# Tokens of a mixture-of-experts layer scattered and gathered once, as doubled rows ordered by pair of keeping experts

## The chip, the cores and the metric

The kernel runs on one core of one Trainium2 chip. The metric is the time of one execution on the device in microseconds; lower is better.

## What is computed

Two layers follow each other on images of 128 channels. The first is a 7x7 depthwise convolution, a norm over the channels and a mixture of eight experts with capacity; the second is an attention by coordinates with a 3x3 convolution, whose input is the first one's output. Cut to what matters here:

```python
x = depthwise_conv7x7(input) + dw_bias             # (32, 128, 56, 56)
x = layernorm(x over channels) * ln_gamma + ln_beta
xf = x.reshape(T, C)                               # T = 100352 tokens, C = 128
topv, topi = top_k(xf @ Wg + bg, 2)                # 8 experts, 2 per token
wts = softmax(topv)
order = argsort(-wts[:, 0])                        # priority
cap = int(1.25 * T / 8)                            # 15680 rows per expert
# in order of priority each expert keeps its first cap tokens
h = gelu(einsum('ecd,edf->ecf', eb, W1) + b1)      # 128 -> 512
y = einsum('ecf,efd->ecd', h, W2) + b2             # 512 -> 128
moe = sum over the 2 picks of y[slot] * gate       # gate 0 where not kept
z = input + x + layer_scale * moe
# second layer, per image: means over rows and columns -> 8 channels ->
# h_swish -> two sigmoids a_h, a_w; conv3x3(z * a_w * a_h), batch norm, SiLU
```

All values are fp32. A token is kept by two experts, by one or by none.

## The kernel before

The program is a row of blocks; each ends with a barrier of all engines. The work of each engine stands in its own function, in order, with semaphores between the engines.

**conv_norm_phase** does the depthwise convolution as matrix products with Toeplitz matrices, stores it to DRAM, reads it back turned, norms it and stores the normed tokens to `xn`, 112 chunks of 896 tokens (128 partitions x `CHK` = 7 tokens of 128 channels). It also leaves the routing logits in SBUF.

**route_phase** finds on DVE the two picks of each token, then by bisection (24 steps, DVE with ACT and PE) the priority that each expert's last kept token has, and by scans the slot of each pick: expert e keeps its tokens in rows e x 15680 and on of `xe`, in order of the chunks. Slots of picks that aren't kept lie outside, and the indirect DMAs leave them out. SP meanwhile fills `xe` with zeros (L504, 16 DMAs). The slots of the first 14 chunks are made first (`early_set`); POOL waits for the zeros and for them, and scatters the first `EARLY` = 8 chunks while DVE makes the other slots. DVE also counts, for each expert and tile of 448 rows, after how many scattered chunks the tile is full (`needed`).

**Scatter.put** (L435) is one chunk's scatter on POOL: wait for the chunk's load, start the load of a later one (L418), then 7 x 2 indirect DMAs, one for each token of a partition and each pick, each of 128 rows of 512 bytes. The last thing in it is the wait for the chunk before to have landed, and the count `chunks_scattered` goes up.

**expert_phase** works on 35 tiles of each expert, 448 rows each, the eight experts in turn: 280 turns, the first and last eight written out and the others in a loop over q with eight turns in its body. POOL scatters the other 104 chunks, with a fill `lull` of 3000 elements after each (L805). SP's queue does, in each turn, `load(t + 5)`: wait for a free buffer, read `needed[q, e]` from SBUF into a register (`value_load`, L823), wait for that many chunks, and one DMA of 224 KB from `xe` (L825); then `store(t)`: wait for the result, one DMA of 224 KB to `ye` (L831). PE's turn is four products up (L875), the turning of the next tile's rows to columns (L866), four products down for the tile before (L883) and the turning back (L892); ACT does the Gelu, DVE the copies out of PSUM.

**output_phase** works on 16 pairs of images, 7 chunks each. POOL gathers for chunk n with 7 x 2 indirect DMAs (L1117) from `ye` into `y_ring`, seven chunks deep; in the first pair it fills the chunk's part of the ring with zeros first (L1113), since rows of tokens that weren't kept aren't written. DVE multiplies by the gates and adds to the normed tokens (L1293), PE turns the chunk (L1170), DVE adds it to the image (L1306); after chunks 3 and 6 come the means, the attention (PE L1180, L1183, L1184; ACT's sigmoid; DVE L1336 and L1338 write `padded`), and PE's 3x3 convolution of the image, seven banks of nine products (L1150), is laid between the next chunks by the list `BEHIND`. The order on every engine is written out by hand.

Of the kernel before, what the change touches and what calls it, by code (L numbers as in the profile page):

```python
# [7 lines left out]
U32 = mybir.dt.uint32  # L8
ALU = mybir.AluOpType
# [3 lines left out]
C = 128  # L13
# [6 lines left out]
E = 8  # L20
# [8 lines left out]
EARLY_PAIRS = 2  # L29
EARLY = 8  # L30
LULL = 3000


def plan(n_images):

    tokens = n_images * HW
    cap = int(1.25 * tokens / E)
    pairs = n_images // 2
    tiles = 35
    tm = cap // (tiles * BLOCKS)  # L40
    assert tm * tiles * BLOCKS == cap and tm <= 128
    return dict(N=n_images, T=tokens, CAP=cap, PR=pairs, J=pairs * KT, TM=tm, TILES=tiles, DROP=E * cap)
# [37 lines left out]
def conv_norm_phase(nc, s, x, dw_kernel, dw_bias, bands, conv, xn, ln_gamma, ln_beta, Wg, bg, logits):  # L80
# [26 lines left out]
    with ExitStack() as ctx:  # L107
# [138 lines left out]
        def _(dve):  # L246
# [20 lines left out]
            def make_hat(m):  # L267
# [17 lines left out]
                dve.tensor_tensor(logits[:, :, m * CHK:(m + 1) * CHK].rearrange("p e j -> p j e"), off[q][:],  # L285
# [113 lines left out]
class Scatter:  # L399


    RING = 7

    def __init__(self, nc, ctx, s, xn, xe, slots):
        sb = lambda name, shape, dt=F32: ctx.enter_context(nc.sbuf_tensor(name, shape, dt))
        sem = lambda name: ctx.enter_context(nc.semaphore(name))
        self.xn, self.xe, self.slots = xn, xe, slots
        self.chunks = s["PR"] * NCHK
        self.chunk = [sb(f"chunk{i}", [128, CHK * C]) for i in range(self.RING)]
        self.chunk_in = [sem(f"chunk_in{i}") for i in range(self.RING)]  # L410
        self.scattered = [sem(f"scattered{i}") for i in range(self.RING)]
        self.chunks_scattered = sem("chunks_scattered")

    def load(self, pool, n):

        g, ch = divmod(n, NCHK)
        i = n % self.RING
        pool.dma_start(self.chunk[i][:], self.xn[g * 128:(g + 1) * 128, ch * CHK * C:(ch + 1) * CHK * C]  # L418
                       ).then_inc(self.chunk_in[i], 16)

    def landed(self, pool, n):

        turn, i = divmod(n, self.RING)
        pool.wait_ge(self.scattered[i], (turn + 1) * 2 * CHK * 16)
        pool.sem_inc(self.chunks_scattered, 1)

    def put(self, pool, n, limit):

        turn, i = divmod(n, self.RING)
# [14 lines left out]
def route_phase(nc, s, logits, xe, slots, gates, needed, scatter):  # L444

    PR, J, CAP, DROP, TILES = s["PR"], s["J"], s["CAP"], s["DROP"], s["TILES"]
# [3 lines left out]
    ZP, ZR, ZD = 98, 80, 16  # L453
    assert ZP * ZR * ZD == E * CAP
    GR = PR * NCHK
    SLICES = ((0, EARLY_PAIRS * NCHK), (EARLY_PAIRS * NCHK, GR))

    with ExitStack() as ctx:
        sb = lambda name, shape, dt=F32: ctx.enter_context(nc.sbuf_tensor(name, shape, dt))
        sem = lambda name: ctx.enter_context(nc.semaphore(name))  # L460
        pick = [sb(f"pick{c}", [128, E, J], BF16) for c in range(2)]
        prio, work = (sb(n, [128, E, J]) for n in ("prio", "work"))
        scan = sb("scan", [128, E * J + 2])
        junk = sb("junk", [128, E, J], BF16)
        zeros = sb("zeros", [ZP, 4 * C])
        top = [sb(f"top{c}", [128, J]) for c in range(2)]
        first, rel = (sb(n, [128, J]) for n in ("first", "rel"))
        ones, below, one_row = sb("ones_r", [128, 128]), sb("below", [128, 128]), sb("one_row", [128, 1])
        bound, low, cand, count, hit, need, minus_mid, enough = (
            sb(n, [128, E]) for n in ("bound", "low", "cand", "count", "hit", "need", "minus_mid", "enough"))  # L470
        flat_logits = logits[:].rearrange("p e j -> p (e j)")
# [925 lines left out]
```

## Time and profile before

| | us |
|---|---|
| median of 3 runs | 5972.66 |
| lowest, highest | 5960.88, 5988.47 |
| span of the profiled execution | 6004.2 |

| engine | busy us | share of the span |
|---|---|---|
| PE | 4869.7 | 81% |
| POOL | 3488.9 | 58% |
| DVE | 2405.2 | 40% |
| ACT | 1512.5 | 25% |

The profile is of one execution, which took 31.5 us more than the median of the runs. The chain that the page shows runs back from the last instruction, at each step to what released it. Instructions of a sequencer (register work, table reads, branches, the issue of DMAs by SP) aren't counted as busy; SP has no row in the table for that reason.

### The profile page before, as it was taken

What the parts mean: (1) busy time and instruction counts of PE and PEld (TensorE: products, weight loads), DVE (VectorE), ACT (ScalarE), POOL (GpSimd) and SP (SyncE); (2) the same over time, 40 slices, a digit from 0 to 9 for tenths busy, and PEclk for the clock granted to TensorE, in tenths of its full rate; (3) what the DMA queues carried; (4) which work ended last, traced back from release to release, by engine and by line L of the source; (5) the groups of instructions that cost most, each with busy time, mean ns of one, the idle gap of its engine ahead of it and who ended that gap; (6) DMA issues with size and microseconds to landing.
All of it is one profiled execution on the core that took longest, in us unless ns stands there. A gap on an engine that the chain in (4) does not pass through costs nothing. (4 is left out here: it accounts for less than half of the span.)

```text
span 6004.2 us, 66408 instructions
## 1 busy us (share of the span) xinstructions
PE 4869.7 (81%) x20680; PEld 2721.7 (45%) x20680; DVE 2405.2 (40%) x4770; ACT 1512.5 (25%) x3688; POOL 3488.9 (58%) x3508
## 2 busy tenths in 40 slices
PE   8999999310399997998779878558888888888888
PEld 3555658310255554544445444224444444444444
DVE  0012226896022222222222222356656556556553
ACT  2233336350033332333223323101111111111111
POOL 0000000004777777877777777477777777777773
PEclk9999999655599998999889989779999999999999
DMA  8887779863333333333223322323333322222310
GB/s 168 185 182 196 194 180 248 260 205 112 96 117 118 118 113 96 94 88 98 84 83 90 93 83 75 118 93 102 105 104 103 107 92 85 82 88 86 101 61 33
DMA packets 840398, 711.26 MB, mean 118 GB/s; under 512 B 596072, under 2 KB 681710, under 8 KB 836090
## 3 DMA queue, kind: packets, MB, share of 16 engines
q1 hardware_dynamic: 666362, 466.30, 28.6%
q0 software_dynamic: 109312, 139.69, 8.5%
q10 hardware_dynamic: 64512, 102.79, 5.0%
q8 instruction: 91, 1.49, 0.1%
q14 instruction: 121, 0.99, 0.0%
HBM read 440.11 MB, written 385.75 MB: 138 GB/s over the span
## 5 line engine op out<-in xcount | busy, mean ns | idle before, releaser
L1117 POOL DMA_INDIRECT y_ring<-ye,index_o x1568 | 1580.7, 1008 | 462.2 <-issue 460.3
L435 POOL DMA_INDIRECT xe<-chunk,slots x1568 | 1536.4, 980 | 476.8 <-issue 476.8
L1150 PE MATMUL cp<-padded,taps_o 128*128 128x448 f32 x4032 | 1627.3, 561 | 62.4 <-DVE padded L1338 62.4
L1150 PEld LDWEIGHTS cp<-padded,taps_o 128*128 128x128 f32 x4032 | 782.1, 198 | 811.8 <-issue 777.6
L921 ACT ACTIVATE hid<-hid_ps,b_cols 128x448 f32<-128x448 f32 x1120 | 709.3, 633 | 1489.6 <-PE hid_ps L875 1391.3
L883 PE MATMUL y_ps<-hid,w_sb 128*128 128x448 f32 x2240 | 932.7, 561 | 0.4 <-DVE yt L946 0.4
L875 PE MATMUL hid_ps<-xt,w_sb 128*128 128x448 f32 x2240 | 890.9, 541 | 1.5 <-DVE xt L940 1.5
L513 POOL MEMSET zeros<- 98x512 f32 x1 | 0.5, 524 | 1109.2 <-POOLq L107 1109.2
L1216 ACT ACTIVATE outb<-cp,shift,s 128x448 f32<-128x448 f32 x224 | 162.1, 724 | 1757.7 <-PE cp L1150 1757.6
L883 PEld LDWEIGHTS y_ps<-hid,w_sb 128*128 128x128 f32 x2240 | 423.1, 199 | 336.4 <-issue 335.8
L1293 DVE SCALAR_TENSOR_TENSOR logits<-y_ring,gates,logits 128x128 f32<-128x128 f32 x1568 | 432.6, 345 | 353.9 <-DMA y_ring<-ye,index_o 336.9
L940 DVE COPY xt<-xt_ps 128x448 f32<-128x448 f32 x280 | 174.8, 624 | 970.3 <-PE xt_ps L866 962.5
L363 PE MATMUL cv<-xin,toep 56*56 56x448 f32 x5376 | 540.0, 543 | 15.8 <-ACT rows L308 9.5
L875 PEld LDWEIGHTS hid_ps<-xt,w_sb 128*128 128x128 f32 x2240 | 404.9, 191 | 315.9 <-issue 311.2
L946 DVE TENSOR_SCALAR yt<-y_ps,b_cols,scale_col 128x448 f32<-128x448 f32 x280 | 208.3, 744 | 691.9 <-PE y_ps L883 691.9
L375 PEld LDWEIGHTS ps<-turner,pix 128*128 128x128 f32 x1568 | 366.8, 326 | 49.1 <-issue 39.9
L375 PE MATMUL ps<-turner,pix 128*128 128x136 f32 x1568 | 378.0, 399 | 8.5 <-DMA pix<-conv 8.5
L1170 PE MATMUL tp<-ident_o,logits 128*128 128x128 f32 x784 | 133.6, 322 | 308.0 <-DVE logits L1293 308.0
L866 PE MATMUL xt_ps<-ident_e,rows_in 112*128 112x112 f32 x1120 | 165.0, 272 | 232.2 <-DMA rows_in<-xe 232.0
L363 PEld LDWEIGHTS cv<-xin,toep 56*56 56x56 f32 x5376 | 224.1, 126 | 284.8 <-issue 262.2
L270 DVE RECIPROCAL rstd<-std 128x7 f32<-128x7 f32 x112 | 22.5, 201 | 818.8 <-ACT std L331 818.8
L1306 DVE SCALAR_TENSOR_TENSOR summed<-tp,beta_o,summed 128x896 f32<-128x896 f32 x112 | 205.4, 1834 | 288.3 <-PE tp L1170 288.2
(198 smaller groups left out, 3627.4 us busy)
## 6 DMA issues: line engine op xcount, KB each, us to landing
xe<-zeros SPq DMA_DIRECT2D x16, 3920.0 KB
rows_in<-xe SPq DMA_DIRECT2D x280, 224.0 KB, 2.7
ye<-rows_out SPq DMA_DIRECT2D x280, 224.0 KB, 2.3
xin<-in_x_dram SPq DMA_DIRECT2D x256, 196.0 KB
conv<-rows ACTq DMA_DIRECT2D x256, 196.0 KB
pix<-conv SPq DMA_DIRECT2D x224, 224.0 KB, 5.1
xn<-hat SPq DMA_DIRECT2D x112, 448.0 KB, 4.3
chunk<-xn POOLq DMA_DIRECT2D x112, 448.0 KB, 3.7
```

The lines of the kernel that those rows point to most:

```text
L363: last = pe.matmul(bank(t, half)[blk * TWO:blk * TWO + H, 0:BW], toep[half * TWO:half * TWO + H, i, kw, :], xin[t % XB][half * TWO:half * ...
L375: last = pe.matmul(tile(m, j), strips[:, j:j + 127 * CHK + 1:CHK], turner[:], start=True, stop=True)
L435: pool.indirect_dma_start(out=self.xe[:, :], out_offset=bass.IndirectOffsetOnAxis(ap=self.slots[:, c, n * CHK + j:n * CHK + j + 1], axis=0 ...
L875: pe.matmul(hid_ps[f][:, 0:NT], w1_sb[e][:, f * 128:(f + 1) * 128], xt[e % 2][:], start=True, stop=True).then_inc(hid_done, 1)
L883: last = pe.matmul(y_ps[:, 0:NT], w2_sb[e][:, f, :], hid[e % 2][:, f, :], start=(f == 0), stop=(f == NH - 1))
L921: act.activation(hid[e % 2][:, f, :], hid_ps[f][:, 0:NT], ACT.Gelu, bias=b1_cols[:, e * NH + f:e * NH + f + 1]).then_inc(hid_ready, 1)
L940: dve.tensor_copy(xt[e % 2][:], xt_ps[e % 2][:, 0:NT]).then_inc(xt_ready, 1)
L946: dve.tensor_scalar(yt[e % 2][:], y_ps[:, 0:NT], b2_cols[:, e:e + 1], scale_col[:, 0:1], ALU.add, ALU.mult).then_inc(yt_ready, 1)
L1117: pool.indirect_dma_start(out=y[ch][c][:, j * C:(j + 1) * C], out_offset=None, in_=ye[:, :], in_offset=bass.IndirectOffsetOnAxis(ap=index[ ...
L1150: last = pe.matmul(cp[i % 2][:, 0:HB * W], taps[:, t, :], padded[b][:, img, hb * HB + kh:hb * HB + kh + HB, kw:kw + W], start=(t == 0), st ...
L1293: last = dve.scalar_tensor_tensor(part, y[ch][c][:, j * C:(j + 1) * C], gates[:, c, bass.ds(n * CHK + j, 1)], part, ALU.mult, ALU.add)
L1306: dve.scalar_tensor_tensor(part, tp[q][:, 0:CC].rearrange("c (k t) -> c k t", k=CHK), beta_c[:, 0:1], part, ALU.add, ALU.add).then_inc(add ...
```

## The change

- The tokens are put into 37 classes: one for each pair of experts a < b that both keep the token, one for each single expert, one for none. Each class fills whole blocks of 128 rows of one DRAM tensor `xy`, whose rows are doubled: 2 x 128 channels. Only each class's last block, and the blocks outside the used ones, are zeroed.
- Each token has one slot. POOL copies a chunk to a doubled one (`twice`), and scatters it with 7 indirect DMAs of 128 rows of 1 KB. Tokens that nobody keeps are scattered too.
- Expert a of a pair reads the left half of a block's rows and overwrites it with its result, expert b the right half. Each expert has up to 130 blocks, taken in the order in which the chunks fill them: 33 tiles of four blocks (the last of two), 512 columns. Where the blocks are stands in a table `where`, read from SBUF, one entry for each block's load and one for its store.
- The output phase gathers each token's row once, 1 KB, and has both results. The gates are exchanged where the second pick is the lower expert (`split_gates`, DVE, in the experts' fifth turn).
- route_phase is rewritten after the bisection: each token's code of keeping experts, flags of the 37 classes, their counts by PE products in bf16, the class starts, the slots of the first 13 chunks, then the table, then the other slots.
- `lull` and the filling of `y_ring` go.

The scatter:

```diff
     def put(self, pool, n, limit):
-        turn, i = divmod(n, self.RING)
-        pool.wait_ge(self.chunk_in[i], (turn + 1) * 16)
-        if n + self.RING - 2 < self.chunks:
-            self.load(pool, n + self.RING - 2)
+        i, d = n % self.STAGED, n % self.DOUBLED
+        pool.wait_ge(self.chunk_in[i], (n // self.STAGED + 1) * 16)
+        if n >= self.DOUBLED:
+            pool.wait_ge(self.scattered[d], (n // self.DOUBLED) * CHK * 16)
+        pool.tensor_copy(self.twice[d][:], self.chunk[i][:].unsqueeze(2).to_broadcast([128, CHK, 2, C])).then_inc(self.copied, 1)
+        pool.wait_ge(self.copied, n + 1)
+        if n + self.STAGED < self.chunks:
+            self.load(pool, n + self.STAGED)
         for j in range(CHK):
-            for c in range(2):
-                pool.indirect_dma_start(
-                    out=self.xe[:, :],
-                    out_offset=bass.IndirectOffsetOnAxis(ap=self.slots[:, c, n * CHK + j:n * CHK + j + 1], axis=0),
-                    in_=self.chunk[i][:, j * C:(j + 1) * C], in_offset=None,
-                    bounds_check=limit, oob_is_err=False).then_inc(self.scattered[i], 16)
+            at = j * self.chunks + n
+            pool.indirect_dma_start(
+                out=self.xy[:, :], out_offset=bass.IndirectOffsetOnAxis(ap=self.slots[:, at:at + 1], axis=0),
+                in_=self.twice[d][:, j, :, :].rearrange("p h c -> p (h c)"), in_offset=None,
+                bounds_check=limit, oob_is_err=False).then_inc(self.scattered[d], 16)
         if n:
             self.landed(pool, n - 1)
```

The experts' loads and stores on SP:

```diff
+                at = [sp.value_load(tables.where[0:1, bass.ds(q * BLOCKS + k, 1), 0, e:e + 1].rearrange("p q e -> p (q e)"),
+                                    min_val=0, max_val=2 * ROWS - 256 + 1) for k in range(blocks)]
-                sp.wait_ge(chunks_scattered, sp.value_load(needed[0:1, bass.ds(q, 1), e:e + 1].rearrange("p q e -> p (q e)"),
+                sp.wait_ge(chunks_scattered, sp.value_load(tables.chunks[0:1, bass.ds(q, 1), e:e + 1].rearrange("p q e -> p (q e)"),
                                                            min_val=1, max_val=PR * NCHK))
-                sp.dma_start(rows_in[i][0:TM, :, :], xe[bass.ds(e * CAP + q * NT, NT), :]
-                             .rearrange("(p k) c -> p k c", k=BLOCKS)).then_inc(tile_in[i], 16)
-
-            def store(t, e, q):
+                for k in range(blocks):
+                    sp.dma_start(rows_in[i][:, k, :], halves[bass.ds(at[k], 256), :].rearrange("(p h) c -> p h c", h=2)[:, 0, :]
+                                 ).then_inc(tile_in[i], 16)
+
+            def store(t, e, q, blocks):
                 i = e % RING
                 sp.wait_ge(out_ready, t + 1)
-                sp.dma_start(ye[bass.ds(e * CAP + q * NT, NT), :].rearrange("(p k) c -> p k c", k=BLOCKS),
-                             rows_out[i][0:TM, :, :]).then_inc(tile_out[i], 16)
+                for k in range(blocks):
+                    at = sp.value_load(tables.where[0:1, bass.ds(q * BLOCKS + k, 1), 1, e:e + 1].rearrange("p q e -> p (q e)"),
+                                       min_val=0, max_val=2 * ROWS - 256 + 1)
+                    sp.dma_start(halves[bass.ds(at, 256), :].rearrange("(p h) c -> p h c", h=2)[:, 0, :], rows_out[i][:, k, :]
+                                 ).then_inc(tile_out[i], 16)
```

The output phase's gather:

```diff
-                    if first:
-
-                        pool.memset(y_ring[:, ch * 2 * CC:(ch + 1) * 2 * CC], 0.0).then_inc(cleared, 1)
-                        pool.wait_ge(cleared, ch + 1)
                     for j in range(CHK):
-                        for c in range(2):
-                            pool.indirect_dma_start(
-                                out=y[ch][c][:, j * C:(j + 1) * C], out_offset=None, in_=ye[:, :],
-                                in_offset=bass.IndirectOffsetOnAxis(ap=index[ch][:, c, j:j + 1], axis=0),
-                                bounds_check=limit, oob_is_err=False).then_inc(y_in[ch], 16)
+                        pool.indirect_dma_start(
+                            out=y[ch][:, j, :, :].rearrange("p h c -> p (h c)"), out_offset=None, in_=xy[:, :],
+                            in_offset=bass.IndirectOffsetOnAxis(ap=index[ch][:, j:j + 1], axis=0),
+                            bounds_check=limit, oob_is_err=False).then_inc(y_in[ch], 16)
```

The new parts of route_phase on which the steps rest (the last block of each class is zeroed by SP for one half of the classes and by ACT for the other; flags and placing on DVE):

```diff
+        def clear_tails(eng, c0, c1):
+
+            for c in range(c0, c1):
+                at = eng.value_load(tails_u[0:1, c:c + 1], min_val=0, max_val=ROWS - 128)
+                eng.dma_start(xy[bass.ds(at, 128), :], zeros[:]).then_inc(zeroed, 16)
...
+            for c0, c1 in SUM_GROUPS:
+                for c in range(c0, c1):
+                    last = dve.tensor_scalar(flags[:, c], code, float(codes[c]), None, ALU.is_equal)
+                last.then_inc(flags_set, 1)
...
+                for c in range(c0, c1):
+                    do(dve.copy_predicated(place[:, :, g0:g1], flags[:, c, :, g0:g1].bitcast(U16),
+                                           ranks[:, c - c0, :].unsqueeze(1).to_broadcast([128, CHK, G])))
```

## Rows read from the trace of the kernel before

**Rows 1.** The page: busy time by engine, and its chain by engine.
```profile
PE 4869.7 (81%) x20680; PEld 2721.7 (45%) x20680; DVE 2405.2 (40%) x4770; ACT 1512.5 (25%) x3688; POOL 3488.9 (58%) x3508
...
POOL 27%; issue 8%; PE 1%; DVE 0%; POOLq 0%; DMA 0%; ACT 0%; ACTq 0%
```

**Rows 2.** Stages: window, length, each engine's busy time (x instructions), clock, DMA.
```profile
0.00:1110.00 1110.00, 1070.57 (x8740) 678.67 (x8740) 281.42 (x1246) 437.05 (x2002) 0.88 (x8) 0.99 0.83 197
1110.00:1419.00 309.00, 42.72 (x134) 33.56 (x134) 284.76 (x542) 103.57 (x210) 6.95 (x28) 0.51 0.66 215
...
1584.00:3835.00 2251.00, 1991.66 (x6786) 1096.45 (x6786) 550.71 (x843) 710.77 (x1122) 1741.98 (x1666) 0.94 0.33 97
3835.00:6004.00 2169.00, 1764.74 (x5020) 913.02 (x5020) 1241.91 (x2087) 261.07 (x355) 1616.55 (x1688) 0.90 0.29 92
```

**Rows 3.** POOL's groups, 1584 to 3770: count | busy, mean ns | idle.
```profile
L435 POOL DMA_INDIRECT xe<-chunk,slots x1456 | 1418.0, 974 | 442.7 <-issue 442.7
L805 POOL MEMSET lull<- 128x3000 f32 x104 | 273.5, 2630 | 0.0
L418 POOL DMA_DIRECT2D chunk<-xn x99 | 59.6, 602 | 0.3 <-issue 0.3
```

**Rows 4.** Waits, 1584 to 3835: total, times, longest.
```profile
PE xt_ps L866 <- DMA rows_in<-xe: 232.0, 24, 27.5
```

**Rows 5.** Timeline of PE, one turn of the experts: start, length.
```profile
1687.15 3.17 PE L875 MATMUL hid_ps<-xt,w_sb 128*128 128x448 f32 x8
1690.16 0.55 PE L866 MATMUL xt_ps<-ident_e,rows_in 112*128 112x112 f32 x4
...
1694.00 3.17 PE L875 MATMUL hid_ps<-xt,w_sb 128*128 128x448 f32 x8
```

**Rows 6.** POOL's groups, 3835 to 6004.
```profile
L1117 POOL DMA_INDIRECT y_ring<-ye,index_o x1568 | 1580.7, 1008 | 462.2 <-issue 460.3 <-POOL y_ring L1113 1.9
```

**Rows 7.** Timeline of PE, output: between two attention products.
```profile
4850.80 0.36 PE L1180 MATMUL ap<-pooled,w_t 128*8 128x112 f32 x2
...
4868.38 13.79 PE L1150 MATMUL cp<-padded,taps_o 128*128 128x448 f32 x36 [1.96 <-DVE padded L1338]
...
4903.94 0.36 PE L1180 MATMUL ap<-pooled,w_t 128*8 128x112 f32 x2
```

**Rows 8.** Timeline of PE: first convolution of the output phase.
```profile
3948.84 15.28 PE L1150 MATMUL cp<-padded,taps_o 128*128 128x448 f32 x36 [5.04 <-DVE padded L1338]
```

**Rows 9.** Timelines: DVE's last early slots, POOL's first load after the zeros.
```profile
1347.64 0.21 DVE L741 TENSOR_SCALAR slots<-rel 128x98 uint32<-128x98 f32 x1
...
1418.18 0.54 POOL L418 DMA_DIRECT2D chunk<-xn  x1 [300.81 <-DMA xe<-zeros]
```

**Rows 10.** Timeline of DVE: bf16 passes, a scan, fp32 passes.
```profile
1124.34 4.17 DVE L600 TENSOR_TENSOR pick<-pick,junk 128x784 bf16<-128x784 bf16 x7
...
1354.04 11.59 DVE L685 TENSOR_TENSOR_SCAN scan<-total,work 128x5488 f32<-128x5488 f32 x1
...
1385.01 6.36 DVE L710 TENSOR_TENSOR work<-work,junk 128x686 f32<-128x686 f32 x8
```

**Rows 11.** Timeline of SP's queue: loads with constant tiles, a store, a load.
```profile
1598.04 4.93 SPq L825 DMA_DIRECT2D rows_in<-xe  x6
...
1702.14 0.33 SPq L831 DMA_DIRECT2D ye<-rows_out  x1
1703.35 0.32 SPq L825 DMA_DIRECT2D rows_in<-xe  x1
```

**Rows 12.** SP's instructions of L823 and L825: count, ns min/median/max.
```profile
L823 SPq FUSED_REGOPS  x544: 46/147/187, 1597.7 to 3798.4; - x182
L823 SPq TENSOR_LOAD <-needed x280: 269/281/975, 1597.2 to 3798.1; - x140
...
L825 SPq DMA_DIRECT2D rows_in<-xe x280: 312/322/350, 1598.0 to 3798.7; - x140
...
DMA to landing us min/median/max: 2.4/2.7/5.9
```

More of the change, by code:

```diff
@@ L38, in plan @@
     pairs = n_images // 2
[L39 to L42, printed above, removed]
+    blocks = (cap + E * 127) // 128
+    assert (TILES - 1) * BLOCKS < blocks <= TILES * BLOCKS and tokens == 784 * 128
+    return dict(N=n_images, T=tokens, CAP=cap, PR=pairs, J=pairs * KT, LAST=blocks - (TILES - 1) * BLOCKS)
 class Steps:
@@ L440, in put, with __init__ @@
         if n:
             self.landed(pool, n - 1)
-def route_phase(nc, s, logits, xe, slots, gates, needed, scatter):
-    PR, J, CAP, DROP, TILES = s["PR"], s["J"], s["CAP"], s["DROP"], s["TILES"]
+class Picks:
+    def __init__(self, nc, ctx, s, gates):
+        sb = lambda name, shape, dt=F32: ctx.enter_context(nc.sbuf_tensor(name, shape, dt))
+        J = s["J"]
+        self.top = [gates[:, c, :] for c in range(2)]
+        self.code, self.code0 = (sb(n, [128, J], BF16) for n in ("code", "code0"))
@@ L450, in route_phase, with __init__, class_of @@
+class Tables:
+    def __init__(self, nc, ctx, s):
+        sb = lambda name, shape, dt: ctx.enter_context(nc.sbuf_tensor(name, shape, dt))
+        self.where = sb("where", [128, POSITIONS, 2, E], U32)
+        self.chunks = sb("chunks_of_tile", [128, TILES, E], U32)
+def class_of(a, b):
+    return a * E - a * (a - 1) // 2 + b - a
+def route_phase(nc, s, logits, xy, slots, picks, tables, scatter):
+    PR, J, CAP = s["PR"], s["J"], s["CAP"]
     GROUPS = 2
@@ new lines, in route_phase @@
+        slots_k = slots[:].rearrange("p (k g) -> p k g", k=CHK)
+        first, rel = (sb(n, [128, J]) for n in ("first", "rel"))
+        place = first[:].rearrange("p (k g) -> p k g", k=CHK)
+        same, inner = (rel[:].bitcast(BF16)[:, i * J:(i + 1) * J].rearrange("p (k g) -> p k g", k=CHK) for i in range(2))
+        ones, ones_b = sb("ones_r", [128, 128]), sb("ones_b", [128, 128], BF16)
+        below_b = sb("below_b", [128, 128], BF16)
+        bound, low, cand, count, hit, need, minus_mid, enough, weight = (
+            sb(n, [128, E]) for n in ("bound", "low", "cand", "count", "hit", "need", "minus_mid", "enough", "weight"))
@@ L580, in _ @@
+            last.then_inc(table_summed, 1)
+            for i in range(len(low_bank), NRG):
+                class_ranks(i)
         @block.vector
@@ L651, in _ @@
             last.then_inc(above_counted, 1)
+            prio_k, pick0_k, junk_k = by_chunk(prio), by_chunk(pick[0]), by_chunk(junk[:])
+            dve.wait_ge(ramps_set, 1)
+            dve.memset(tab, 0.0)
+            dve.memset(inner[:, 0, :], 0.0)
+            dve.memset(place, 0.0)
+            do(dve.memset(ahead[:, :, 0, :], 0.0))
+            for e in range(E):
+                last = dve.tensor_scalar(tie[:, e], prio_k[:, e], bound[:, e:e + 1], 2.0 ** e, ALU.is_equal, ALU.mult)
+            last.then_inc(ties_set, 1)
@@ new lines, in rank_within, with set_slots @@
+            def rank_within(g0, g1):
+                for d in range(1, CHK):
+                    out = inner[:, 1:, g0:g1] if d == 1 else same[:, 0:CHK - d, g0:g1]
+                    do(dve.tensor_tensor(out, code[:, d:, g0:g1], code[:, 0:CHK - d, g0:g1], ALU.is_equal))
+                    if d > 1:
+                        do(dve.tensor_tensor(inner[:, d:, g0:g1], inner[:, d:, g0:g1], same[:, 0:CHK - d, g0:g1], ALU.add))
+            def set_slots(g0, g1):
+                do(dve.tensor_tensor(slots_k[:, :, g0:g1], place[:, :, g0:g1], inner[:, :, g0:g1], ALU.add))
@@ L973, in output_phase @@
-def output_phase(nc, s, x, xn, ye, ln_beta, slots, gates, logits, out, p):
+            scale(end - 1, E - 1, False, LAST * 128)
+            result(end - 2, E - 2, TILES - 1, False, LAST)
+            result(end - 1, E - 1, TILES - 1, False, LAST)
+def output_phase(nc, s, x, xn, xy, ln_beta, slots, gates, logits, out, p):
     PR, N = s["PR"], s["N"]
```

680 lines of the change are left out of this document (435 added, 245 removed).

## The prediction

> **What bounds the kernel now.** I read the page first, for the order of things: PE is busy 81% of the span, and yet the chain that ended last is mostly POOL's, on one line, the gather of the output phase [rows 1]. Then the busy time by stage [rows 2]: the first 1110 us (convolution and norm) are PE's and are left alone by the change; then come the routing (1110 to 1419), POOL's first eight puts, which close the route block (1419 to 1584), the experts (1584 to 3835, 2251 us) and the output (3835 to 6004, 2169 us).
>
> Experts: POOL's groups in that stage show 1456 indirect scatters of 0.974 us with 0.30 us of issue between them, and 104 fills `lull` of 2.63 us [rows 3]. 104 chunks x (14 x 1.28 + 2.63 + 0.4) = 104 x 21.0 = 2180 us, and PE's only large wait is for tiles that the scatter had not filled, 232 us [rows 4]. A turn of PE is 6.85 us when it doesn't wait [rows 5], 280 x 6.85 = 1918. So the scatter sets this stage's end, with PE 15% behind. Output: 1568 gathers of 1.008 us at a pitch of 1.30 [rows 6], 14 per chunk, 112 x 18.4 = 2060 us of 2169. PE needs less: between two attention products, in a half pair in which nothing waited for a gather, lie 53.1 us [rows 7], about 107 us for a pair where gathering takes 129.
>
> **The output phase.** Each chunk now takes 7 gathers, 7 x 1.30 + 0.4 = 9.5 us, 33 us for half a pair against PE's 53: POOL leaves the path and PE's own order of work is what is late next. First convolution: it starts at 3948.8 now [rows 8], 114 us into the stage, behind four chunks of 20 us (the ring's fills of 1.5 us go too). With 9.5 us each it starts 74 us in. From there PE has 32 images x 48.0 (7 banks of 6.86), 107 chunks' transposes x 0.77 = 82, 31 attention products x 0.87 = 27, the wait of about 1.9 us per image for `padded` that the rows show, 57 [rows 7], and 10 before the last image: 1712, and 4 at the end. 74 + 1712 + 4 = 1790 against 2169: **-379 us**. Bounds: if DVE's and ACT's turns hold a pair at 115 instead of 107 us, -250; below 107 it can't go, as PE's work is the same.
> Does one gather of 1 KB rows cost what one of 512 B rows does? No row shows 1 KB rows. The scatter and the gather take 0.97 and 1.0 us whatever lies in their slots, so I take 1.0, the nearest rows; upper end twice that (a rival below).
>
> **The route block.** The zeroing of `xe` (62 MB) goes, and POOL waited for it until 1418.2, although DVE had the early slots at 1347.9 [rows 9]. In its place DVE must finish all classes' counts before the first slot. Working on from the end of the search (1319.4), with a bf16 pass of 784 at 0.6, a fp32 pass of 686 at 0.80 and a scan at 2.1 ns an element [rows 10]: 16 compares 9, `ahead` 4, tie run 3, `taken` 6.4, two bf16 passes 8, `code` 3.5, 37 flags x 0.3 = 11, the wait for PE's and ACT's class sums 16 (it hides `inner` and `code0`), block arithmetic 6, 37 predicated copies x 0.3 = 11: 78, so slots at about 1398, then the 36 tail clears, 18 on SP and 18 on ACT at 0.92, overlap it and end near 1404. POOL then makes 8 puts; each is 7 x 1.28, the load 0.9 and the doubling copy. No row shows a copy on POOL; it writes 1792 elements, 1.6 us at the fill's rate [rows 3], at most some 4: I take 2.5, and 15 us for a put while DVE works beside it. 1404 + 120 + 9 for the end of the block = 1533; DVE's late part (scan 9, table 45, 37 copies x 0.9 = 34) ends near 1490, under it. The experts start **51 us earlier**; bounds -80 and +20, as half of these operations have no row of their own.
>
> **The experts, PE's side.** Blocks are full 128 rows, 130 per expert: 8 x 130 x 128 = 133120 columns against 125440. The eight large products of a turn are 6.02 us for 448 columns [rows 5], so 6.88 for 512, and the transposes 0.85: 7.7 us a turn, 256 of them and 8 of half size, 2000 us, 80 more than before. The scatter: a put is 7 x 1.28 + 0.9 + 2.5 = 12.4 us, 104 puts in 1290 us; the `lull` goes. It no longer holds PE.
>
> **The experts, SP's side.** This is what is late next. SP did one table read and two DMAs a turn; now it does nine reads and eight DMAs, all in one in-order queue: a tile's load is four block loads, its store four block stores, each with its own address from `where`. What one costs is in SP's timeline: from a store's issue to the next load's issue, with one table read between them and nothing to wait for, 1.21 us in the loop (1702.14 to 1703.35), and 0.92 us where the tile number is a constant (six loads issued in 4.93 us, the last taking 0.32: 4.61/5) [rows 11]. The parts are there too: the read 0.28, its check 0.147 at the median, the DMA itself 0.32 [rows 12]. A block thus costs between 0.92 and 1.21; I take 1.16, near the loop's value, since addresses come from the loop's register, less a little because the new reads' lower limit is 0. A turn: 8 x 1.16 + 0.62 for the ninth read = **9.9 us, more than PE's 7.7**. The cover that hid SP's work before (it waited most of each 6.85 us) is gone. Sum of the stage: 14 for the weights' DMAs, 21 for the first five loads, 8 turns with constants x 7.9 = 63, 240 in the loop x 9.9 = 2376, again 63, the half turns 22, the end 10: 2569 against 2251, **+318 us**. Store waits don't add to it: a store comes five loads behind its own tile. The scatter's count is ready: eight tiles take 79 us and need 3.4 chunks, 42 us.
>
> The Trainium skill, DMA: Bandwidth & Descriptors, section on latency and other measured facts, puts a floor of about 600 ns under a table read (`tensor_load`). The trace disagrees: 281 ns at the median of 280 [rows 12]; with 600 the turn would be 12.8 us. The same page, under issuing engines that are not separate queues, says that the time to start a DMA is usually small beside the DMA itself, which speaks against an SP bound; of one DMA that holds here too, 0.32 us of issue and 2.7 to landing [rows 12]. Eight of them overlap in landing and not in issue, so I weigh the issue.
>
> **Other parts.** The new order of `logits` and `slots` changes strides only, 0 (off DVE's path in the first 1110 us). Splitting the gates is 11 short DVE operations in the fifth turn of the experts: DVE is busy 551 of 2251 us [rows 2], 0. Half-row blocks make four DMA pieces of each 2 KB one; the DMA engines are 33% busy in that stage [rows 2], 0 on the path. The clock: a PE that waits 2 us a turn may be granted less; it was granted 0.94 in this stage with long waits [rows 2], and at 0.9 a turn is still under 9.9.
>
> **Sum.** -51 + 318 - 379 = -112 us on the profiled 6004.2. The median of the runs is 5972.7, 31.5 below the profile, so 5973 - 112 = **5861 us**, -1.9%.
>
> **Rivals.**
> A, slower: SP's turn is dearer. At 1.21 a block, with the ninth read at 0.66 and 0.3 a turn for the loop's branch and the fetch of a body five times as long (SP's dearest read took 975 ns where the median is 281 [rows 12]), it is 10.6 us: +170, **6031 us**. For it: the loop rows are those of the same queue. Against: that row has a check against two limits. Slower than before begins at 9.9 + 112/240 = 10.4 us a turn.
> B, SP is cheap: at 0.92 a block, 7.9 us, SP and PE are level. -2.0 x 240 = -480, **5380 us**. For it: the constant-address rows; against: only where no register is needed.
> C, a doubled row costs twice: scatter 1.94, gather 2.0 us. Puts in the route block +54; in the experts 104 x 19.3 = 2010, hidden by SP; the gather 112 x 16.4 + 105 = 1940 against 1790, +150: **6065 us**. Against it: a load of 3.5 KB rows on the same engine costs POOL 0.60 us [rows 3], so the bytes of a row aren't what POOL pays for.
> D, PE's order isn't as tight as in the half pair I read: 115 us a pair, +128, **5989 us**, no change.
> E, the table read at the skill's 600 ns. Worked out from rows it is a read twice as long: its dearest, 975, is rare; at 281 + 300, 9 x 0.3 = 2.7 more a turn, +648, **6509 us**. The skill's figure (page above) is about that.
> F, the change doesn't shorten POOL's gather, because dropped tokens, which were skipped, are now fetched: the count of instructions, not of rows, sets 1.3 us, so this is C in small, and is in it.
>
> **Chances.** Forecast 62% (own range 5740 to 5985), A 17%, B 8%, C 5%, D 7%, E 1%. A measurement tells about 0.5%, 30 us, from no change. Faster: 0.55 of the forecast, B, 0.01 of D: 0.64. Within: 0.05 of the forecast, 0.02 of A, 0.05 of D: 0.12. Slower: 0.02 of the forecast, 0.15 of A, C, E and 0.01 of D: 0.24. To leave no more than 2 in 10 out, the range goes from 5640 (a turn of 9.0) to 6080 (through A and C).
>
> **What would show it.** In the profile after: SP's DMA issues in the experts' loop without a gap, turns of 9.9 us, PE waiting about 2 us in each for `rows_in` and no longer for POOL; the scatter done some 1000 us before the stage ends; in the output phase POOL idle half of the time, pairs of 107 us and the chain on PE; the first scatter near 1404 and the experts' start near 1533. Wrong: turns of 7.7 with PE at work throughout (B), indirect DMAs near 2 us (C), or a route block past 1600.

## The result, and the profile after

The changed kernel takes 7259 us (7256 to 7261, four runs) against 5967 (5957 to 5988): a ratio of **1.215 [1.212, 1.219]**. It is much slower, where 5861 was forecast and the range ended at 6080. The profiled execution has a span of 7257.9 us, 1254 more than the one of before.

The page of the kernel after, busy time by engine and the chain by engine (beside [rows 1]):

```profile
PE 5066.4 (70%) x20517; PEld 2657.6 (37%) x20517; DVE 2421.7 (33%) x4879; ACT 1540.1 (21%) x3769; POOL 1893.5 (26%) x1983
...
PE 20%; DVE 4%; issue 1%; ACT 1%; ACTq 0%
```

POOL has 1983 instructions where it had 3508 and is off the chain, as meant. Busy time by stage, same columns as [rows 2]; the lines are the norm, the route block, POOL's early puts, a stretch that before did not have, the experts' turns, and the output:

```profile
0.00:1110.00 1110.00, 1069.97 (x8740) 678.29 (x8740) 281.63 (x1246) 438.27 (x2002) 0.89 (x8) 0.99 0.84 197
1110.00:1419.00 309.00, 62.79 (x263) 40.27 (x264) 296.65 (x641) 121.89 (x355) 61.12 (x83) 0.55 0.17 58
1419.00:1541.00 122.00, 23.03 (x193) 19.41 (x192) 54.05 (x104) 0.00 (x0) 91.91 (x92) 0.50 0.44 147
1541.00:2722.00 1181.00, 26.19 (x68) 12.17 (x68) 4.98 (x7) 12.17 (x17) 915.92 (x901) 0.51 0.35 117
2722.00:5447.00 2725.00, 2198.88 (x6236) 1034.76 (x6236) 549.84 (x796) 706.29 (x1040) 0.00 (x0) 0.94 0.17 50
5447.00:7258.00 1811.00, 1685.50 (x5020) 872.70 (x5020) 1234.60 (x2087) 261.50 (x355) 823.67 (x900) 0.96 0.43 143
```

From 1541 to 2722 hardly anything but POOL works: PE is busy 26 of 1181 us. The waits of SP's queue (in total, times, longest) name the reason, and PE's timeline shows its two holes:

```profile
SPq L1064 <- POOLq L434: 1180.1, 2, 735.9
```

```profile
1966.66 1.08 PE L1109 MATMUL xt_ps<-ident_e,rows_in 128*128 128x128 f32 x4 [429.25 <-DMA rows_in<-xy]
...
1990.90 3.60 PE L1117 MATMUL hid_ps<-xt,w_sb 128*128 128x512 f32 x8
2722.26 1.12 PE L1109 MATMUL xt_ps<-ident_e,rows_in 128*128 128x128 f32 x4 [727.77 <-DMA rows_in<-xy]
```

SP waits twice for `chunks_scattered` (POOL's increments, L434). It has read the table for its first tile at 1518 and may load it at 1962.8; three tiles follow at once, and the fifth, expert 4's first, comes at 2718.9. POOL's scatters up to the first of these moments, and in all (count: ns min/median/max, first and last start):

```profile
L448 POOL DMA_INDIRECT xy<-twice,slots x331: 971/976/1332, 1402.6 to 1961.5; - x166
```

```profile
L448 POOL DMA_INDIRECT xy<-twice,slots x784: 968/976/1332, 1402.6 to 2716.2; - x196
```

At seven scatters a chunk, 331 are 47 chunks and a little of the 48th; the last of the 784 starts at 2716.2, 2.6 us before the fifth tile's load. So the table asked for 47 of 112 chunks for the first tile and for **all 112** for the fifth. In the kernel before, PE waited 232 us in all for tiles [rows 4], and SP 530.7 us, in 27 waits, for the same count:

```profile
SPq L825 <- POOLq L425: 530.7, 27, 39.2
```

Between the waits and the output lies SP's queue. Its timeline over a round of eight turns (start, length; the lines between are alike):

```profile
3398.21 1.94 SPq L1064 DMA_DIRECT2D rows_in<-xy  x4
3401.08 3.92 SPq L1073 DMA_DIRECT2D xy<-rows_out  x4
3408.82 1.94 SPq L1064 DMA_DIRECT2D rows_in<-xy  x4
...
3470.45 1.96 SPq L1064 DMA_DIRECT2D rows_in<-xy  x4
3473.33 3.87 SPq L1073 DMA_DIRECT2D xy<-rows_out  x4
3483.58 1.94 SPq L1064 DMA_DIRECT2D rows_in<-xy  x4
```

3398.21 to 3483.58 is 85.4 us for eight turns, **10.67 us a turn**: seven of 10.3 on average and, at the loop's end, one of 13.1. SP has no gap in them, and PE waits about 2 us in each (1675.8 us of waits for `rows_in` less the two holes is 519, over 238 turns).

### The profile page after: what moved, and what is told of

Read it like the earlier page. It is cut to its first block and busy times, and to the rows that moved or that the text cites. A ratio compares the mean times of both kernels' runs of the same rounds, so it can differ in the third digit from the quotient of the medians.

```text
span 7257.9 us, 77541 instructions
## 1 busy us (share of the span) xinstructions
PE 5066.4 (70%) x20517; PEld 2657.6 (37%) x20517; DVE 2421.7 (33%) x4879; ACT 1540.1 (21%) x3769; POOL 1893.5 (26%) x1983
## 3 DMA queue, kind: packets, MB, share of 16 engines
q0 software_dynamic: 84224, 257.01, 10.9%
## 5 line engine op out<-in xcount | busy, mean ns | idle before, releaser
L1413 PE MATMUL cp<-padded,taps_o 128*128 128x448 f32 x4032 | 1578.3, 547 | 62.5 <-DVE padded L1601 62.5
L1109 PE MATMUL xt_ps<-ident_e,rows_in 128*128 128x128 f32 x1040 | 182.4, 300 | 1676.3 <-DMA rows_in<-xy 1675.8
L1167 ACT ACTIVATE hid<-hid_ps,b_cols 128x512 f32<-128x512 f32 (+1 forms) x1056 | 717.2, 681 | 2748.5 <-PE hid_ps L1117 2747.0
L1125 PE MATMUL y_ps<-hid,w_sb 128*128 128x512 f32 (+1 forms) x2112 | 1078.6, 660 | 0.4 <-DVE yt L1192 0.4
L1186 DVE COPY xt<-xt_ps 128x512 f32<-128x512 f32 (+1 forms) x264 | 180.4, 684 | 2516.9 <-PE xt_ps L1109 2516.9
L1117 PE MATMUL hid_ps<-xt,w_sb 128*128 128x512 f32 (+1 forms) x2112 | 939.2, 587 | 3.0 <-DVE xt L1186 3.0
L1380 POOL DMA_INDIRECT y_ring<-xy,index_o x784 | 799.2, 1019 | 244.2 <-issue 241.1
L448 POOL DMA_INDIRECT xy<-twice,slots x784 | 770.0, 982 | 255.9 <-issue 255.1
L1109 PEld LDWEIGHTS xt_ps<-ident_e,rows_in 128*128 128x128 f32 x1040 | 117.0, 148 | 1887.2 <-DMA rows_in<-xy 1453.9
L1192 DVE TENSOR_SCALAR yt<-y_ps,b_cols,scale_col 128x512 f32<-128x512 f32 (+1 forms) x264 | 211.7, 802 | 833.4 <-PE y_ps L1125 833.4
```

Source lines behind the costliest of these rows:

```text
L448: pool.indirect_dma_start(out=self.xy[:, :], out_offset=bass.IndirectOffsetOnAxis(ap=self.slots[:, at:at + 1], axis=0), in_=self.twice[d][ ...
L1109: last = pe.transpose(xt_ps[e % 2][:, k * 128:(k + 1) * 128], rows_in[e][:, k, :], ident[:])
L1117: pe.matmul(hid_ps[f][:, 0:cols], w1_sb[e][:, f * 128:(f + 1) * 128], xt[e % 2][:, 0:cols], start=True, stop=True).then_inc(hid_done, 1)
L1125: last = pe.matmul(y_ps[:, 0:cols], w2_sb[e][:, f, :], hid[e % 2][:, f, 0:cols], start=(f == 0), stop=(f == NH - 1))
L1167: act.activation(hid[e % 2][:, f, 0:cols], hid_ps[f][:, 0:cols], ACT.Gelu, bias=b1_cols[:, e * NH + f:e * NH + f + 1]).then_inc(hid_ready, 1)
L1192: dve.tensor_scalar(yt[e % 2][:, 0:cols], y_ps[:, 0:cols], b2_cols[:, e:e + 1], scale_col[:, 0:1], ALU.add, ALU.mult).then_inc(yt_ready, 1)
```

## The experiments

The theory, **O**: the two long waits come from the order in which the changed table puts blocks into tiles. Two things differ from before. In the kernel before, an expert with fewer rows than its capacity had them at the end of its places, and the absent ones first:

```python
do(dve.tensor_scalar(spare[:], lower[:, 0, 0:E], -1.0, float(CAP), ALU.mult, ALU.add))   # before, L657
do(dve.tensor_scalar(spare[:], spare[:], 0.0, None, ALU.max))
do(dve.tensor_tensor(expert_base[:], expert_base[:], spare[:], ALU.add))
```

The change drops `spare`: positions are counted from 0 and absent blocks come last. And it sorts an expert's blocks by the fraction of *their class* that they end at, as if every class grew evenly over the chunks. The data of `setup_inputs`, put through the reference's routing, are neither even nor balanced: expert 4 keeps 578 tokens and expert 5 keeps 1713 of 15680 places, and for 59% of all tokens the first weight is exactly 1.0, so the ties are kept in the order of tokens. Experts 6 and 7 are chosen by 67276 and 59960 tokens and are full early; only from then on do tokens of the pair (0, 6) or (0, 7) count as kept by 0 alone. That class, of the tokens that expert 0 holds alone, has 7082 tokens and the smallest fractions, and so the first position, though it fills late: none of its tokens lies in the first 40 chunks. Worked out from this data by the table's rule, expert 0's first tile needs 47 chunks and expert 4's 112, the two counts that the profile shows. The rival, **S**: the scatter itself is late for any tile.

For SP's turn, theory **Q** is that SP's own queue sets it. Its rivals are **L**, that PE waits for the loads to land however soon SP issues them, and **G**, that work moved to ScalarE holds up the Gelus.

The first four kernels, and the same kernels again beside the changed one (e9 to e12), ran on chips on which the kernel before takes 6680 us; the comparison above, e5 to e8 and e13 to e16 ran on chips on which it takes 5970 to 6020. Times are compared within a session; only e3 and e7 are set against runs of the changed kernel in another session, on a chip of the same kind. e5, e6, e7 and e13 are one execution each.

**Absent positions first, and the lone class later** (the lone class of expert e is (e, e), the tokens that only e keeps). In the table code of the changed kernel:

```diff
+ do(dve.tensor_reduce(absent[:], neg_blocks[:], AX_X, ALU.add))
+ do(dve.tensor_scalar(absent[:], absent[:], float((TILES - 1) * BLOCKS + s["LAST"]), None, ALU.add))
+ do(dve.tensor_tensor(pos[:], pos[:], absent[:].unsqueeze(2).to_broadcast([128, E, E]), ALU.add))
```

> The changed kernel with one thing different in its table: an expert with fewer blocks than its 130 positions has its absent positions first, as the kernel before had them (its 'spare'), so that the few blocks of experts 4 and 5 stand in the last rows of tiles. Theory O (order of the tiles): SP's wait of 736 us ahead of the fifth tile goes, since that tile is expert 4's first and waited for chunk 112 of 112; the wait of 444 us ahead of the first tile stays nearly (chunk 45 in place of 47, 23 us less). Sum 7259 - 713 - 23 = 6523 us. Theory S (the scatter itself is late, and whatever SP asks for waits for its end): the same two waits, 7259 us.

6738 us, 1.0085 [1.0044, 1.0127] of the kernel before. One wait for the scatter is left on SP's queue, as O says:

```profile
SPq L1068 <- POOLq L434: 418.9, 1, 418.9
```

The second kernel adds to this that the blocks of class (e, e) are sorted as if `held` more of them, 2/3 of their number, stood ahead:

```diff
+ do(dve.tensor_scalar(held[:], alone(neg_blocks[:]), -2.0 / 3, MAGIC, ALU.mult, ALU.add))
+ do(dve.tensor_scalar(held[:], held[:], MAGIC, None, ALU.subtract))
+ do(dve.scalar_tensor_tensor(alone(rows_v[:]), held[:], 128.0, alone(rows_e[:]), ALU.mult, ALU.add))
...
+     last = dve.scalar_tensor_tensor(ahead_n[:, e, e, :], rows_v[:, e, :], held[:, e:e + 1], ahead_n[:, e, e, :],
+                                     ALU.mult, ALU.add)
...
+     last = dve.tensor_scalar(ahead_q[:, e, :, e], ahead_q[:, e, :, e], held[:, e:e + 1], None, ALU.add)
```

> As e1_absent_first, and in addition the blocks of the tokens that an expert holds alone are placed later among its blocks (as if 2/3 as many blocks of them stood ahead), because these tokens come late in the order of chunks, when the other expert of the pair is full. Theory O: both long waits for the scatter go, since no tile of the table is asked for ahead of its chunks at a turn of 10.2 us; the sum is 7259 - 1123 = 6136 us, and SP's turn of 10.1 us is what is left between the first tile and the last. Theory S: 7259 us. If only the fifth tile's wait is the order's: 6520 us as e1_absent_first.

6407 us, 0.959 [0.954, 0.963]; no wait for the scatter is on SP's list. Against S both times. The sizes are off on this chip, 215 us in e1 and 271 in e2, which the last session settles.

**Half the stores on ScalarE** (`HALF` is 2; ScalarE calls `store_rest` behind its four Gelus, for the tile three turns back).

```diff
-                for k in range(blocks):
+                for k in range(HALF):
...
+            def store_rest(t, e, q):
+                act.wait_ge(out_ready, t + 1)
+                for k in range(HALF, BLOCKS):
+                    at = act.value_load(tables.where[0:1, bass.ds(q * BLOCKS + k, 1), 1, e:e + 1].rearrange("p q e -> p (q e)"),
+                                        min_val=0, max_val=2 * ROWS - 256 + 1)
+                    act.dma_start(halves[bass.ds(at, 256), :].rearrange("(p h) c -> p h c", h=2)[:, 0, :], rows_out[e][:, k, :]
+                                  ).then_inc(tile_out[e], 16)
```

> The changed kernel with two of the four stores of a tile, and their two table reads, moved from SP to ScalarE, behind its four Gelus and three tiles late. Theory Q (SP's queue sets the turn of 10.1 us): SP's turn falls by 2 x 1.19 = 2.4 us to 7.8 us, beside PE's own 7.75 us; some 256 turns x 2.3 us = 590 us less, 6670 us. Rival L (the landing of the loads sets the turn, PE's 1.4 to 1.9 us of idle ahead of the transposes): no change, 7259 us. Rival G (ScalarE's 2.4 us of issuing delay the Gelus that PE needs): a turn over 10.1 us and more than 7259 us.

6756 us, 1.011 [1.006, 1.016]. Its waits for chunks are those of the changed kernel; its turns aren't. First e3's waits; then, in the columns of [rows 2], the stretch behind the second wait, above in the changed kernel on a chip of the same kind (e9) and below in e3:

```profile
SPq L1067 <- POOLq L434: 1178.5, 2, 733.6
```

```profile
2722.00:5449.00 2727.00, 2234.85 (x6236) 1062.18 (x6236) 549.71 (x796) 706.24 (x1040) 0.00 (x0) 0.92 0.17 50
2719.00:4854.00 2135.00, 2042.04 (x6236) 1000.26 (x6236) 550.10 (x796) 706.56 (x1040) 0.00 (x0) 0.98 0.22 64
```

592 us less (the first profile had 2725 there too), with PE busy 96% of the time: Q, by the size that was expected. The total, 6756, is 86 us above the expected 6670; the changed kernel itself takes 90 us more on such a chip than the 7259 from which that was worked out. L and G fall.

> e2_order and e3_two_queues together. Theories O and Q: the two add, the turn is 7.9 us from the first tile on, and the waits for chunks are below 60 us in sum: 7259 - 1123 - 550 = 5590 us, below the kernel before (5967 us). If the scatter, which takes until 2719 us, is slowed by or slows the tiles beside it: 5700 to 5900 us. Theory S: no less than 6670 us.

5897 us, 0.883 [0.879, 0.887], faster than the kernel before; each gain is there beside the other. It lies in the range for tiles and scatter that slow each other (5700 to 5900), and not at 5590.

**The kernel before, given the changed kernel's order.**

```diff
-            do(dve.tensor_scalar(spare[:], spare[:], 0.0, None, ALU.max))
+            do(dve.tensor_scalar(spare[:], spare[:], 0.0, None, ALU.mult))
```

> The kernel before with its 'spare' set to nothing, so that an expert with few tokens has them in its first tiles and the absent rows behind them, as the changed kernel has. Its table of needed chunks then asks for chunk 87 or so ahead of expert 4's first tile and for chunk 112 ahead of its second. Theory O (the order of rows in the tiles is what made the changed kernel wait): the kernel before gets the same wait, until its last chunk at about 3770 us; 268 tiles of 8.0 us and the output's 2170 us stand behind it, 8080 us in place of 5967. Theory S (the changed kernel's doubled scatter or its table made the wait, whatever the order): no change, 5967 us.

7771 us in its one execution, where the session's kernel before took 5983:

```profile
SPq L825 <- POOLq L425: 2123.8, 2, 1650.6
```

```profile
1584.00:3753.00 2169.00, 93.67 (x299) 51.07 (x299) 23.09 (x36) 34.15 (x53) 1719.92 (x1636) 0.52 0.14 41
3753.00:5600.00 1847.00, 1836.16 (x6430) 1010.94 (x6428) 531.93 (x806) 678.60 (x1069) 4.59 (x9) 1.00 0.23 67
```

This one line, without doubled rows, blocks or a new table, turns SP's 530.7 us of waits for the count into 2123.8 and makes the same hole, until 3742 us, where the last chunks land. The time is 310 us under the expectation because the tiles behind the hole take 6.9 us, not 8.0: nothing is left for them to wait for, and the granted clock is 1.00.

> The kernel before, unchanged, with a profile from the same chip as the other three, since its time was 6680 us on the chip of the runs above and 5967 us on the first: by stages, the difference lies in the output stage, where one more 500 to 700 us are waited for transfers, and not in the stage of the experts.

The premise fell in that session: it took 6002 us, with 2251 us of experts and 2165 us of output, as in [rows 2]. Where the 700 us of the other chips lie in the kernel before, no run shows.

**The gather in halves** (`index` holds twice the slot, `odd` one more).

```diff
-                            out=y[ch][:, j, :, :].rearrange("p h c -> p (h c)"), out_offset=None, in_=xy[:, :],
-                            in_offset=bass.IndirectOffsetOnAxis(ap=index[ch][:, j:j + 1], axis=0),
+                        for h in range(2):
+                                out=y[ch][:, j, h, :], out_offset=None, in_=halves[:, :],
+                                in_offset=bass.IndirectOffsetOnAxis(ap=(index, odd)[h][ch][:, j:j + 1], axis=0),
```

> The changed kernel with the output's gather of a doubled row (1 KB) made as two gathers of 512 B each, so that a pair of images has 98 of them again, of the same bytes. If the gain of the output stage (2169 to 1810 us) is that GpSimd issues half as many gathers: 98 x (1.02 + 0.32) = 131 us for a pair in place of 107 (PE), 16 x 24 = 380 us more, 7640 us. If it is something else (contiguity, the place of the rows in memory): no change, 7259 us.

7638 us, 379 more than the changed kernel took (380 expected), and all of it behind 5446 us, where the output stage begins as before (5447). POOL's two groups, and the page's chain by engine:

```profile
L1386 POOL DMA_INDIRECT y_ring<-xy,index_o x784 | 790.0, 1008 | 221.9 <-issue 221.0
L1386 POOL DMA_INDIRECT y_ring<-xy,odd_o x784 | 787.4, 1004 | 238.9 <-issue 238.6 <-PE tp L1439 0.3
```

```profile
POOL 21%; issue 6%; PE 1%; DVE 0%; POOLq 0%; DMA 0%; ACT 0%; DVEq 0%; ACTq 0%
```

The output stage is 2190 us for 1811, near the 2169 of the kernel before, and the chain is back on POOL. The same bytes in twice the instructions give up the whole gain, so the gain in this stage is the count of POOL's instructions.

**Three stores on ScalarE.** e4_both with `HALF = 1`.

> e4_both with three of the four stores of a tile on ScalarE in place of two. In e4_both the turn was 11.1 us while the scatter ran (1520 to 2720 us) and 8.33 us behind it, where PE was busy for 862 of 900 us. Theory Q (SP's queue, slowed by GpSimd's own issuing, sets the turn while the scatter runs): 1.2 us or more less for each of some 108 turns, 130 us less than e4_both, which was 0.883 of the kernel before; and no change behind the scatter, where PE sets the turn. Rival G (ScalarE, which then issues 3.6 us beside 2.8 us of Gelus, becomes the bound): no gain or a loss in either part.

5457 us, 0.912 [0.908, 0.915] of a kernel before of 5983. Behind the scatter the turn is 7.75 us (e16 below shows it) where e4_both's was 8.33, against what I expected: PE's 96% in e3 had not been its limit. The two kernels ran on chips of different kinds here; e15 and e16 set them side by side.

**The four again, on one chip.**

> The changed kernel, unchanged, on the chip of the three that follow, so that the four can be set against each other: the runs e1 to e4 were made on a chip on which the kernel before took 6680 us, and where single instructions of SP's queue took 0.6 to 0.7 us each while the scatter ran. Where that is not so: 7259 us, ratio 1.215.

7349 us, 1.1005 [1.093, 1.109] of 6678: again a chip of the other kind. 90 us more than on the first chip, of which 81 are in the output stage (1892 against 1811).

> e1_absent_first again. By the turn of 10.66 us that the traces show over whole rows of tiles (10.13 us and 4.2 us more at the end of each round of eight): first tile at 1937 us, 264 turns to 4752, output 1811: 6563 us on a chip without the disturbance.

> e2_order again. First tile at 1517 us, 264 turns of 10.66 us to 4331, output 1811: 6142 us. If the turn of 13 us that e2_order had while the scatter ran belongs to the kernel (GpSimd's issuing beside SP's) and not to that chip: 110 turns x 2.4 us more, 6400 us.

> e4_both again. SP's turn with two stores is 10.13 - 2.38 + 0.53 = 8.28 us over whole rows: 1520 + 264 x 8.3 + 1811 = 5522 us, and so 65 us or more above e8_three_stores (5457 us), whose turn is PE's 7.75 us. If PE set the turn in both: the same as e8_three_stores.

6736, 6409 and 5896 us, each within 2 us of its first run. Against e9: -613, -941 and -1453. e10 and e12 miss their 6563 and 5522 by 173 and 374 us, and e11 comes out where the slow turn would belong to the kernel (6400): on these chips alone that could not be told from a property of the chip.

**The last session: what belongs to the chip.**

> The kernel before, unchanged, for its stages on the chip of the three that follow. If it takes 5970 us: as the first profile. If it takes 6680 us: the 700 us lie where GpSimd's indirect transfers run (scatter and gather), since the changed kernel, which has half as many, takes only 90 us more there (7349 against 7259).

> e2_order again. On a chip where the kernel before takes 5970 us: 1517 + 264 x 10.66 + 1811 = 6142 us. If the turn of 13 us beside the scatter belongs to the kernel: 6400 us there too.

> e4_both again. On a chip where the kernel before takes 5970 us: 1520 + 264 x 8.33 + 1811 = 5530 us; if the turn of 11 us beside the scatter belongs to the kernel: 5810 us there too.

> e8_three_stores again, beside e15_both on one chip. SP's turn over whole rows is 8.3 us with two stores left and 7.1 us with one, and PE's own 7.75 us: 8.3 - 7.75 = 0.55 us for each of 264 turns, 145 us less than e15_both. If PE sets both: no difference.

Kernel before 5980 us with a profile, 6013 in the session's other runs. e14 takes 6134 us (6142 expected), 1.020 [1.016, 1.024]; e15 5592, 62 above its 5530 and far from 5810, 0.930 [0.926, 0.934]; e16 5454, 0.907 [0.904, 0.910], which is 138 us less than e15 where 145 was expected. The stretch of the experts beside the scatter in e11 (other chip) and in e14 (same kernel), and SP's loads in them (count: ns min/median/max):

```profile
1520.00:2720.00 1200.00, 860.14 (x2287) 410.56 (x2288) 203.37 (x289) 256.37 (x374) 931.34 (x917) 0.88 0.49 157
```

```profile
1520.00:2720.00 1200.00, 959.74 (x2705) 457.78 (x2706) 238.78 (x340) 306.34 (x445) 934.53 (x918) 0.93 0.52 165
```

```profile
L1081 SPq MOVE rows_in<-xy x272: 1/29/708, 1705.7 to 2589.7; - x136
```

```profile
L1081 SPq MOVE rows_in<-xy x328: 29/29/38, 1705.8 to 2596.0; - x164
```

The first and third line are e11's, the others e14's. On e11's chip single instructions of SP, a register move too, take up to 0.71 us while POOL scatters, and in 900 us 272 block loads are issued in place of 328; on e14's no register move takes over 0.04 us. So the turn of 13 us, which e2 and e11 had beside the scatter, was the chip's. In e14, rid of both waits, PE still waits 600 us in 246 waits for `rows_in`, none over 6.6 us: SP's turn. In e16 that is gone too, 71.5 us in five waits, and a turn is 7.75 us (PE's timeline):

```profile
3101.99 3.60 PE L1136 MATMUL hid_ps<-xt,w_sb 128*128 128x512 f32 x8
...
3109.74 3.60 PE L1136 MATMUL hid_ps<-xt,w_sb 128*128 128x512 f32 x8
...
3117.48 2.74 PE L1136 MATMUL hid_ps<-xt,w_sb 128*128 128x512 f32 x6
```

## Why the prediction was wrong

Its three stages against the profiles, as differences from before:

| | forecast | measured |
|---|---|---|
| route block (to SP's first transfer of the experts, 1584 before) | -51 | -85 (1499) |
| experts (2251 before) | +318 | +1697 (1499 to 5447) |
| - of it the waits for the scatter | 0 | +1180 |
| - of it SP's turn and the rest | +318 | +517 |
| output (2169 before) | -379 | -358 |
| sum | -112 | +1254 |

**The step that failed** is the last sentence of SP's side: "The scatter's count is ready: eight tiles take 79 us and need 3.4 chunks, 42 us." It took an average for a table. The average pace was right: a put takes 11.6 us, so the 85.4 us of eight turns hold 7.4 chunks, twice the 3.4 that were needed. But what each tile waits for is set by the slowest block in it, and the table that says so was rewritten by the change. The term was put at nothing and measured 1180 us in two waits. [Rows 4] showed a wait of 232 us for tiles, and I read it as a property of the scatter's pace alone; how long a tile waits depends on the order of rows as well, as e5 shows, where one line of the kernel before turns SP's 530.7 us of such waits into 2123.8. That line, with `spare`, stood among the removed lines of the diff, and the prediction prices neither it nor the new sort. No rival held this case, so the range ended 1180 us below the result. Two questions would have found it: which tile is loaded first, and what is the last chunk that has a row in it; and is the data of `setup_inputs` even over experts and over tokens. Of the two waits, the absent positions first give back 613 us (e9 to e10) and the lone class later 328 (e10 to e11); that is less than the 736 and 419 us of SP's waits, because the tiles that now run beside the scatter took 12.6 to 13.2 us each on that chip, and 10.67 behind it.

**SP's turn: right in mechanism, a size off.** SP bounds the experts' stage, as forecast: no gap in its queue, and two of its stores moved to another queue give back 592 us of the stage in e3. The term was 9.9 us and is 10.67. A store's block costs 1.19 for 1.16 ([rows 11] had 1.21, and the lower limit of 0, for which I took less, saves nothing: the check is 0.152 us at the median as in [rows 12]); and a round of eight turns ends with 2.8 us more, which I had left to rival A. A named both and said 10.6. With the waits out of the way, something close to A is what happened: e14 is slower than the kernel before by 2.0% [1.6, 2.4], and the prediction has slower begin at "10.4 us a turn". The forecast had given A 17%. Its 6134 us are 103 above A's 6031. By stages 80 of them are the experts' (2819 us from 1499 to 4318, where A has 2251 + 318 + 170): about 30 are turns of 10.9 to 11.0 us in place of 10.67 while the scatter runs, 17 are 10.67 in place of 10.6, and the rest the rounds with constants, whose turns take 9.7 us and not 7.9 (2732.97 to 2800.76 in the changed kernel is seven of them), and a start 20 us before the first load where I had 14. The output is 21 over and the route block 34 under. Most of the 36 us left are the 31.5 that the profile of before took beyond its median: A took them off, and e14's profiled execution (6131) has no such excess.

**PE's side: right.** 7.7 us a turn was forecast and e16, where little else is late (71.5 us), has 7.75.

**The route block: right in direction.** First put at 1398.6 (1404 forecast), but 11.6 us a put and not 15 (the first took 13.2), since the copy of 1792 elements takes 1.70 us and not 2.5. In the changed kernel SP's earlier start buys nothing, as it only waits longer for the scatter; in e14 it does.

**The output: right.** 1811 for 1790: first convolution 80 us into the stage (5527.3) for 74, and 1731 behind it for 1716. POOL is off the chain. e7 restores 98 gathers a pair and the stage is 2190 us: the term was the number of instructions.

**The other rivals.** C (a doubled row costs twice) is out: the page has 0.982 us in the mean for a scatter of 1 KB rows, and [rows 3] 0.974 for 512 B; a gather takes 1.02 for 1.01 [rows 6]. B and D didn't occur. E is out by 1040 reads of the load's table in the changed kernel:

```profile
L1059 SPq TENSOR_LOAD <-where x1040: 260/266/589, 1515.3 to 5429.5; - x174
```

The floor of about 600 ns that the Trainium skill gives (DMA: Bandwidth & Descriptors, latency and other measured facts) is more than twice this median; these reads are from SBUF, and the page doesn't say which memory it means. The same page of the Trainium skill (issuing engines are not separate DMA queues) says that starting DMAs on several engines "will only save the time on the sequencer it takes to initiate the DMA, which is usually small relative to the DMA itself". The runs agree with the first half and limit the second: a load's block lands 1.8 us after its issue in the median, but eight addresses, reads and issues in one queue are 10 us, and moving half the stores away is worth 542 us (e14 to e15).

**What beats both kernels.** e8_three_stores, 5457 us, 0.912 and 0.907 of the kernel before in its two sessions: the doubled rows as changed, absent positions first, the lone class later, and one of four stores left on SP.

## What to carry to other kernels

A consumer that waits for a producer's count is only as early as the least ready element it asks for first; when a change touches the order in which work is laid out, work out that need for the first tiles, from the real data, before trusting an average pace. And when work moves from few large transfers to many small ones with addresses from a table, count instructions of the issuing queue: here one block is 1.2 us of SP, and the bytes matter little: the issue itself is 0.34 us for 64 KB where it was 0.32 for 224 KB [rows 12]. Look in a diff at the lines that are removed as closely as at those that are added: a term such as `spare` shows no cost in the profile of before because it is there.

## What the runs showed of the hardware

An indirect transfer of 128 rows keeps GpSimd busy for 0.97 to 1.02 us, for rows of 1 KB as for rows of 512 B, for scatter and gather. A transfer on SP's queue whose address comes from a table costs 1.19 us of it: read 0.27, check 0.15 and 0.02, address 0.07, issue 0.34, the rest between them. The end of the loop over eight turns costs SP's queue some 2.8 us. And the same program differs between chips by more than most of the effects studied: the kernel before takes 5970 to 6020 us or 6680, the changed one 7259 or 7349, with single instructions of SP up to 0.71 us beside GpSimd's scatter on the slower ones (e11). Why is open; a comparison needs both kernels on one kind of chip, best in one session.
